# Conv attention, linear attention and a mixture of experts on one core: the group norm's deviation as one product, epsilon in VectorE's copy, and products of zeros at the opening

## The reference

```
h  = group_norm(x, 32 groups of 4 channels, eps 1e-6) * scale + bias
x  = x + Wp . softmax((Wq h)^T (Wk h) / sqrt(128)) . (Wv h)         # 1024 tokens, one head
t  = tokens of x                                                    # [1024, 128] per image
t  = t + linear_attention(layer_norm(t)) @ W_out + b_out            # 4 heads of 32
t  = t + sum over 8 experts of share_e * (gelu(n @ w1_e + b1_e) @ w2_e + b2_e) + n,  n = layer_norm(t)
```

## Time and profile before

| | |
|---|---|
| median of 3 runs | 318.69 us (318.09 to 318.78) |
| span of the profiled execution | 315.6 us |
| outside the span (median less span) | 3.1 us |
| PE busy | 297.7 us, 94% |
| DVE busy | 254.9 us, 81% |
| ACT busy | 200.8 us, 64% |
| POOL busy | 154.1 us, 49% |

### The profile page before, as it was taken

How to read it: one execution, slowest core, us unless ns; L and a number is a source line. 1 busy time by engine, 2 the same in 40 slices (tenths; PEclk the granted TensorE clock), 3 DMA queues, 4 the chain that set the end, 5 groups by cost and what they waited for, 6 DMA issues and landing times.

```text
span 315.6 us, 5504 instructions
## 1 busy us (share of the span) xinstructions
PE 297.7 (94%) x1584; PEld 238.3 (76%) x1584; DVE 254.9 (81%) x635; ACT 200.8 (64%) x352; POOL 154.1 (49%) x358
## 2 busy tenths in 40 slices
PE   5898989989999999999999999998799998999996
PEld 4776768866878887878887797875677786668885
DVE  4599686587587799987698887999598896999996
ACT  3447474566771587663279577468578645888882
POOL 2899593059941985980784300599604049200000
PEclk9999999999999999999999999999999999999999
DMA  5902000010000021000000118395321783229801
GB/s 136 330 12 70 0 1 2 0 66 2 1 3 0 0 69 39 30 12 0 0 1 0 66 38 271 117 391 212 124 86 67 279 300 119 75 87 375 295 7 66
DMA packets 12904, 29.61 MB, mean 94 GB/s; under 512 B 2208, under 2 KB 6224, under 8 KB 10960
## 3 DMA queue, kind: packets, MB, share of 16 engines
q1 hardware_dynamic: 12448, 28.87, 26.3%
q10 hardware_dynamic: 432, 0.46, 0.4%
HBM read 24.73 MB, written 4.59 MB: 93 GB/s over the span
## 4 chain that ended last, share of the span: by engine, by line
PE 66%; DVE 13%; POOL 9%; ACT 7%; issue 3%; DMA 1%; DVEq 0%; POOLq 0%
PE ring L1464 11%; PE ring L1449 7%; PE ring L1451 7%; PE ring L1450 7%; PE scores L1449 6%; PE scores L1451 6%; PE scores L1450 6%; POOL w_n L589 3%; PE ring L1805 3%; POOL u L589 3%; ACT pT_hi L726 3%; ACT prob L720 2%; PE ring L1604 2%; DVE pT_lo L1059 2%; PE ring L1591 2%
## 5 line engine op out<-in xcount | busy, mean ns | idle before, releaser
L867 ACT ACTIVATE gel<-scores,b_c 128x512 f32<-128x512 f32 x64 | 43.9, 689 | 19.5 <-PE scores L1451 18.0
L1059 DVE TENSOR_TENSOR pT_lo<-ring,pT_hi 128x512 fp32r<-128x512 f32 x64 | 40.5, 681 | 9.8 <-ACT pT_hi L726 9.4
L720 ACT ACTIVATE prob<-prob,row_max 128x1024 f32<-128x1024 f32 x32 | 36.8, 1149 | 14.2 <-DVE prob L1052 14.2
L580 POOL TENSOR_SCALAR rstd<-lmv 128x4 f32<-128x4 f32 x16 | 4.3, 266 | 82.3 <-DVE lmv L1094 81.1
L1052 DVE TENSOR_SCALAR_CACHE_REDUCE prob<-scores 128x1024 f32<-128x1024 f32 x32 | 38.6, 1214 | 3.3 <-PE scores L1451 3.3
L726 ACT ACTIVATE pT_hi<-ring 128x512 fp32r<-128x512 f32 x64 | 34.6, 599 | 10.3 <-PE ring L1464 9.9
L1464 PE MATMUL ring<-ident,prob 128*128 128x128 f32 x256 | 33.7, 275 | 3.6 <-ACT prob L720 1.9
L1464 PEld LDWEIGHTS ring<-ident,prob 128*128 128x128 f32 x256 | 28.7, 140 | 8.5 <-ACT prob L720 3.7
L1449 PE MATMUL scores<-wT_hi,w_hi 128*128 128x512 f32 x64 | 29.3, 458 | 0.0
L1449 PE MATMUL scores<-k_both,q_hi 128*128 128x512 f32 x64 | 26.9, 421 | 1.9 <-DVE k_both L1037 1.3
L1449 PE MATMUL ring<-pT_hi,v_hi 128*128 128x512 f32 x64 | 26.5, 415 | 0.8 <-DVE pT_lo L1059 0.8
(11 more groups left out here) (300 smaller groups left out, 780.9 us busy)
## 6 DMA issues: line engine op xcount, KB each, us to landing
pT_hi<-scratch_s SPq DMA_DIRECT2D x8, 1024.0 KB, 7.6
prob<-scratch_s SPq DMA_DIRECT2D x4, 1024.0 KB, 7.2
k_both<-scratch_s SPq DMA_DIRECT2D x3, 1024.0 KB, 5.8
z_in<-scratch_z SPq DMA_DIRECT2D x8, 256.0 KB, 2.9
out_dram<-out_s SPq DMA_DIRECT2D x7, 256.0 KB, 2.2
xb<-in_x_dram SPq DMA_DIRECT2D x3, 512.0 KB, 3.3
scratch_z<-out_s SPq DMA_DIRECT2D x2, 512.0 KB, 2.8
k_both<-scratch_s SPq DMA_DIRECT2D x4, 256.0 KB, 4.2
```

Of the source, the lines that this page charges most:

```text
L720: act.activation(prob[:, i % 2, :], prob[:, i % 2, :], ACT.Exp, bias=row_max[:, i:i + 1], scale=-1.0, accum_out=row_sum[:, 0, i:i + 1]).th ...
L867: act.activation(half(gel, s % 2), scores[:, s % 2, :], ACT.Gelu, bias=b1_c[:, s % E:s % E + 1]).then_inc(e_gelu, 1)
L1059: dve.tensor_tensor(tile_group(pT_lo, n, i), as_tiles(ps(place, unit)), tile_group(pT_hi, n, i).bitcast(FP32), ALU.subtract).then_inc(drai ...
```

## The change

Four edits.

1. A new matrix `group_dev`, identity less `group_mean`, is made by DVE at the start, in a part of t2. `group_means` multiplies both matrices by the channel means: column 0 on is now the deviation itself, column 4 on the group mean. For image 0 DVE squares the deviation and adds the variance in one instruction that reads PSUM; for images 1 to 3 it takes three. The copy of the group mean moves behind.
2. Epsilon is added by DVE in its copy of the group variance; POOL's addition goes.
3. `keep_busy` multiplies `router_two` by `router_top` (fp32r, zeros) in place of `group_mean` and `ident`.
4. The fill counts change: 36 products as soon as the zeros are there, in place of 4 behind `const_made`; 2 in place of 1 ahead of `group_variances`; 4 new ones behind it; 3 in place of 1 in `merge_values`; 4 in place of 1 after it.

```diff
             def group_rstd(place, b0, nb):
                 wait_drained(pool, place, "gn_var")
-                after(pool.tensor_scalar(gsum[:, 3, b0:b0 + nb], gsum[:, 2, b0:b0 + nb],
-                                         1.0, GN_EPS, ALU.mult, ALU.add))
-                pool.tensor_tensor(gsum[:, 3, b0:b0 + nb], gsum[:, 3, b0:b0 + nb],
+                pool.tensor_tensor(gsum[:, 3, b0:b0 + nb], gsum[:, 2, b0:b0 + nb],
                                    minus_half[:, 0:nb], ALU.pow).then_inc(gn_rstd, 1)
...
             def group_deviation(place, b0, nb):
-                mean, dev = gsum[:, 0, b0:b0 + nb], gsum[:, 1, b0:b0 + nb]
+                dev, unit = gsum[:, 1, b0:b0 + nb], ps(place, "gn_mean")
                 wait_filled(dve, place, "gn_mean")
-                dve.tensor_copy(mean, ps(place, "gn_mean")[:, 0:nb]).then_inc(drained[place.bank("gn_mean")], 1)
-                wait_drained(dve, place, "gn_mean")
-                after(dve.tensor_tensor(dev, gmv[:, b0:b0 + nb, 0], mean, ALU.subtract))
-                after(dve.tensor_tensor(dev, dev, dev, ALU.mult))
-                dve.tensor_tensor(dev, dev, gmv[:, b0:b0 + nb, 1], ALU.add).then_inc(gn_mv, 1)
+                if nb == 1:
+                    dve.scalar_tensor_tensor(out=dev, in0=unit[:, 0:1], scalar=unit[:, 0:1], in1=gmv[:, b0:b0 + 1, 1],
+                                             op0=ALU.mult, op1=ALU.add).then_inc(gn_mv, 1)
+                else:
+                    after(dve.tensor_copy(dev, unit[:, 0:nb]))
+                    after(dve.tensor_tensor(dev, dev, dev, ALU.mult))
+                    dve.tensor_tensor(dev, dev, gmv[:, b0:b0 + nb, 1], ALU.add).then_inc(gn_mv, 1)
+                dve.tensor_copy(gsum[:, 0, b0:b0 + nb], unit[:, B:B + nb]).then_inc(drained[place.bank("gn_mean")], 1)
...
             def group_variance(place, b0, nb):
                 wait_filled(dve, place, "gn_var")
-                dve.tensor_copy(gsum[:, 2, b0:b0 + nb], ps(place, "gn_var")[:, 0:nb]
-                                ).then_inc(drained[place.bank("gn_var")], 1)
+                dve.tensor_scalar(gsum[:, 2, b0:b0 + nb], ps(place, "gn_var")[:, 0:nb], GN_EPS, None, ALU.add
+                                  ).then_inc(drained[place.bank("gn_var")], 1)
...
-            dve.memset(router_top[:, :].bitcast(FP32), 0.0)
+            dve.memset(router_top[:, :].bitcast(FP32), 0.0).then_inc(zeros_made, 1)
+            dve.wait_ge(const_made, 1)
+            dve.tensor_tensor(group_dev, ident[:, :], group_mean[:, :], ALU.subtract).then_inc(dev_made, 1)
...
             def group_means(place, n, b0, nb):
                 pe.wait_ge(gn_mv, n + 1)
-                small(place, "gn_mean", nb, group_mean[:, :], gmv[:, b0:b0 + nb, 0])
+                dst, means = open_unit(place, "gn_mean"), gmv[:, b0:b0 + nb, 0]
+                pe.matmul(dst[:, 0:nb], group_dev, means, start=True, stop=True)
+                fill(place, "gn_mean", pe.matmul(dst[:, B:B + nb], group_mean[:, :], means, start=True, stop=True))
...
                 for _ in range(products):
-                    pe.matmul(scores[:, 0, 0:C], group_mean[:, :], ident[:, :], start=True, stop=True)
+                    pe.matmul(scores[:, 0, 0:C], router_two[:, :], router_top[:, :], start=True, stop=True)
...
                 turn(SETUP, "wvT", [wv_s[:, :]])
-                keep_busy(1)
+                keep_busy(3)
...
+            pe.wait_ge(zeros_made, 1)
+            keep_busy(36)
             pe.wait_ge(const_made, 1)
+            pe.wait_ge(dev_made, 1)
+            group_means(SETUP, 0, 0, 1)
+            keep_busy(2)
+            group_variances(SETUP, 0, 0, 1)
             keep_busy(4)
-            group_means(SETUP, 0, 0, 1)
-            keep_busy(1)
-            group_variances(SETUP, 0, 0, 1)
             merge_values()
-            keep_busy(1)
+            keep_busy(4)
```

More of the change, by code:

```diff
@@ L237, in conv_attention_moe @@
         wv_s, wp_s, wvT = gT_s, ctx_s, m2T_s
+        group_dev = t2[:, 0, :]
         w1_raw, w2_raw = t1[:, :, :].rearrange("p a b -> p (a b)"), w2_s[:, :]
@@ L268, in conv_attention_moe @@
         const_made = sem("const_made")
+        zeros_made, dev_made = sem("zeros_made"), sem("dev_made")
         mask_made = sem("mask_made")
@@ L944, in group_deviation, with group_affine @@
             def group_deviation(place, b0, nb):
-                mean, dev = gsum[:, 0, b0:b0 + nb], gsum[:, 1, b0:b0 + nb]
+                dev, unit = gsum[:, 1, b0:b0 + nb], ps(place, "gn_mean")
                 wait_filled(dve, place, "gn_mean")
-                dve.tensor_copy(mean, ps(place, "gn_mean")[:, 0:nb]).then_inc(drained[place.bank("gn_mean")], 1)
-                wait_drained(dve, place, "gn_mean")
-                after(dve.tensor_tensor(dev, gmv[:, b0:b0 + nb, 0], mean, ALU.subtract))
-                after(dve.tensor_tensor(dev, dev, dev, ALU.mult))
-                dve.tensor_tensor(dev, dev, gmv[:, b0:b0 + nb, 1], ALU.add).then_inc(gn_mv, 1)
+                if nb == 1:
[6 more added lines that the diff above has]
+                dve.tensor_copy(gsum[:, 0, b0:b0 + nb], unit[:, B:B + nb]).then_inc(drained[place.bank("gn_mean")], 1)
             def group_variance(place, b0, nb):
                 wait_filled(dve, place, "gn_var")
-                dve.tensor_copy(gsum[:, 2, b0:b0 + nb], ps(place, "gn_var")[:, 0:nb]
-                                ).then_inc(drained[place.bank("gn_var")], 1)
-            def group_affine(n, b0, nb):
+                dve.tensor_scalar(gsum[:, 2, b0:b0 + nb], ps(place, "gn_var")[:, 0:nb], GN_EPS, None, ALU.add
+                                  ).then_inc(drained[place.bank("gn_var")], 1)
+            def group_affine(place, n, b0, nb):
                 dve.wait_ge(gn_rstd, n)
+                wait_drained(dve, place, "gn_mean")
                 after(dve.tensor_scalar(gmul[:, b0:b0 + nb], gsum[:, 3, b0:b0 + nb], gs_c, None, ALU.mult))
@@ L983, in first_weights @@
                 dve.wait_ge(ld_w["gn"], 32)
+                wait_drained(dve, SETUP, "gn_mean")
                 g = gmul[:, 0:1]
@@ L1241, in opening_batch @@
                 invert_sums(b, 0)
-                group_affine(2, 1, B - 1)
+                group_affine(place, 2, 1, B - 1)
                 weights_again()
```

## The result

The changed kernel takes 323.83 us, the median of 6 runs (322.83 to 324.65); before it was 318.43 in its 6 (317.08 to 319.15). The ratio is 1.015, with a 95% interval of 1.0119 to 1.0181: slower by 1.5%. I had forecast 318.5. The time lies above my range and on the other side of before, and close to the rival "zeros don't lift the clock", 323.0, to which I had given 0.16.

The account below looks back on a forecast made before the run. The opening's chain up to DVE's q_lo was taken as the bound: 1.84 us lost ahead of the group means, 2.0 gained behind, -0.15 net. Span 315.6 becomes 315.45, plus 3.1 around it: 318.5 us, range 316.7 to 321.0.

Parts of the forecast that it names:

- zeros don't lift the clock: Slower rival for the opening: clock stays low through the fills, group means start at 8.92, total 323.0 us; chance 0.16.
- when the clock rises: Opening step: PE reaches the upper clock 4.8 us into the fills, at 6.1 us, halving the time of the remaining fills.
- T: Time in the opening at which PE's clock rises to the upper level; taken as 6.1 us.
- the sum: Opening total: 1.84 us lost ahead of the group means, 2.0 gained behind them, shift -0.15 us.
- A fill is bound by its load: Opening fills: each narrow fill takes its load's time, 0.213 us at the lower clock and 0.107 at the upper.
- The first rival: Opening: loads hide, a fill takes 0.107 us at the lower clock, group means stay at 5.69; total 316.9; chance 0.26.
- M = T/2 + 4.48: Opening: formula for when the fills end and the group means start; 7.53 us with T at 6.1.
- M: Time in the opening at which PE starts on the group means; 5.69 us before, 7.53 forecast.
- The leg behind M at the upper clock: Stretch from M to q_lo, 7.51 us before, claimed 2.0 us shorter with PE at the upper clock.
- DVE's and POOL's gain: Group arithmetic in the opening: gmul starts at M + 2.45 instead of 3.18, 0.73 us earlier.
- Hidden edits: DVE's making of the new matrix at about 3.07, some 0.2 us, is hidden ahead of x's arrival at 4.08.
- A shift at q_lo reaches the end: A microsecond gained or lost at q_lo (13.20 us) counts as one at the kernel's end.

Follow-up runs that it names:

- e3: Changed kernel with fills of 512 columns of fp32r zeros, 18, 1, 2, 1, 2 in place of 36, 2, 4, 3, 4; ratio to before 1.0004.
- e2: Changed kernel with fills as fp32 products of the same zeros, 18, 1, 2, 1, 2 of them; ratio to before 1.0013.
- e4: Changed kernel with the same narrow fp32r fills and counts, but of the constant 1.5 instead of zeros; ratio to before 1.0143.
- e7: Changed kernel with 20 narrow fills at the opening instead of 36; ratio to before 1.0026.
- e8: Kernel before with only the new narrow fills of zeros and their counts, group arithmetic untouched; ratio to before 1.0158.
- e6: Changed kernel with 512-column zero fills, 9 at the opening, plus 7 between q1 and the first scores; ratio to before 0.9961.
- e1: Kernel before with only the new group arithmetic (deviation by one product, epsilon on DVE), fills as before; ratio to before 0.9977.
- e9: Kernel before with 3 and 8 products of 512 columns added in the tail, where PE waits for POOL's u; ratio to before 0.9962.
- e11: e10 with its zeros made first, 10 opening fills instead of 9 and fewer fills behind M; ratio to before 0.9893, median 315.79 us.
- e10: e6 with the tail fills of e9 added; ratio to before 0.9932.
- e5: Changed kernel with 512-column zero fills, 9 at the opening, none added ahead of the first scores; ratio to before 0.9963.

## Why the prediction was wrong

The step that failed is "when the clock rises". I placed the rise 4.8 us into the fills, at T = 6.1, because before's had come as far into a stretch without a pause, and gave 0.50 to it. In the changed kernel it came only near 20 us, where the distance of products falls from 0.42 to 0.23, after q0, k0, k1 and nearly all of q1. So neither half of the sum held: the group means start at 9.00 and not at 7.53, and the leg behind them takes 8.65 us and not 5.5.

I treated a narrow fill as equal to the work in before's stretch. There, from 8.38 to 13.2, PE had six products of 512 columns, among fp32 products of 128 columns and of one. A narrow fp32r fill is bound by its load: 0.215 us, about twice the 0.107 that I estimated for its product. After 36 of them the clock was still at the lower level; among wide or fp32 fills of about the same total time it rose (e3, e2). I had named the possibility in the rival, and argued against it by the word "pause". The rows showed starts of loads and products and could not bear that word out.

Point by point:

- *A fill is bound by its load:* right, 0.215 us measured for 0.213; e4, e7 and e8 show the same. The first rival (0.107) is refuted at the lower clock, and with it, for fp32r at that clock, the figure that the Trainium skill (TensorE: Matmul & The Clock Gate, LDWEIGHTS) gives.
- *M = T/2 + 4.48:* not met in the changed kernel, as no rise came within the fills; M was 9.00, for 8.92 in the rival.
- *The leg behind M at the upper clock, 5.5 us (7.51 less 2.0):* nearly right in e3 (5.63) and e6 (5.70). At the lower clock the changed kernel needs 8.65, 1.14 more than before; the rival's +1.1.
- *DVE's and POOL's gain, 0.73 us at gmul:* 2.73 from M to gmul against 3.18, 0.45 gained. I had put it at the upper clock, where e3 shows 2.18 for my 2.45. Of the half microsecond removed from DVE only 0.16 shows at the copy with epsilon (M + 1.89 for M + 2.05). It does not count in the changed kernel anyway, since q0 waits for PE (e1: 0.15 at q_lo).
- *Hidden edits:* the new matrix took 0.29 us at 3.07, ahead of x at 4.12: right.
- *A shift at q_lo reaches the end:* right. From image 0's first exponential to the last at 190 us, the exponentials of the attention stand 4.3 to 4.6 us later than before's.

I also misread the clock row. I wrote that the slices don't resolve the slow opening, but a finer window of before reads 1.00 as well, though q0's products in it are 0.43 us apart:

```profile
9.00:12.00 3.00, 3.00 (x14) 2.71 (x13) 1.46 (x7) 0.54 (x2) 2.17 (x5) 1.00 1.00 322
```

So in these profiles the row does not show the lower level ahead of the first rise, and the distances have to be read there. The mean granted clock of a run leaves out the opening too: before's profile has a mean of 1.000. One later stretch of 3.4 us at the lower level makes 0.995 of it.

The spans of the two profiles differ by more than this shift, 6.6 us, and the rest can be placed. About 0.5 us is at 193 to 199 us, where DVE waits 1.73 us for a load of the experts' shares (`k_both<-scratch_s`) instead of 0.81; e1 and e9 wait as long, so the fills don't cause it. 1.6 us is the fall of the clock in the tail, which before's profile lacks. All six runs of the changed kernel have a granted clock of 0.995 or less, so each should have had such a fall. The medians differ by 5.4; but before's 6 runs beside the changed kernel were quick. In the later groups its median is 318.94 to 319.46, and e4 and e8, slow in the opening like the changed kernel, are 4.3 and 4.6 us above it.

From q_lo to the end e8 and e11 took 303.9 and 304.0 us without a fall of the clock, before and e4 302.4 and 302.2. Those 1.5 us arise in the experts from about 205 us on, ahead of the tail's u: POOL's layer norm takes longer there (the first scaling to `w_n` 1.47 us instead of 0.45), so that the first u comes 3.3 us later in e8 and 2.9 in e11 than the shift at q_lo accounts for. PE waits 2.4 and 2.1 us for `w_n`, a wait that before does not have. Why POOL is slower in some executions stays open.

The range was also too narrow at the top: it ended at 321.0, below the 323.0 of a rival to which I had given 0.16.

## What to carry to other kernels

A filler product on PE has to be judged by its load as well as by its columns. Here 128 columns of fp32r cost the load's 0.215 us each, and the clock did not rise among them in any of the four profiles that have them (the changed kernel, e4, e7, e8). With 512-column products it rose within or right behind the opening's fills in three profiles of five (e3, e6, e10, not e5 and e11). Fit the number of fills to the time at which the real operand arrives, counted at the lower clock, and keep those behind it few, because if the rise fails each of them stands on the path. And look for waits of PE of 2 us in the middle of a kernel, ahead of dense work: filling the tail's was worth as much here (e9, 1.2 us) as all the wide fills of the opening (e5, 1.2 us).

## What the runs showed of the hardware

- The clock's rise is no fixed time of a kernel: e5 and e6 give PE the same work up to q1, and e6 had q0's products at the upper level from 9 us, e5 at the lower until about 17.
- A wait of PE of 1.8 us (e2, 14.9 to 16.7) or of 0.8 and 2.1 us with four turned tiles between (the tail) can be followed by some 3.4 us at the lower clock. In most profiles this begins behind the wait, in the dense work (0.8 us behind in e2, 1.4 behind the tail's in e5); in e6 it begins at 220.5, 0.3 us before PE goes on. In the tail it cost 1.6 to 1.8 us where it came.
- Zeros did not hold the clock down: it rose among zeros in two forms (e2, e3) and did not among a constant in the narrow form (e4). Varied values were not run.
